# A decoder layer: the context's maxima, its rounding jobs and the zero fill are dealt out to other steps of the attention

## The reference, cut to what matters

```python
x = x + attn(layernorm(x))            # 32 query heads, 8 key/value heads, causal, rotary
x = x + xattn(layernorm(x), ctx)      # below
x = x + moe(layernorm(x))             # top-1 of 8 experts with a capacity, and a shared expert

def xattn(x, weight):                 # E, M, K = 4, 512, 512
    # both operands are rounded to 8 bits and back before the product
    xq = per 1x128 block:   (x * 448/amax).astype(fp8) * amax/448
    wq = per 128x128 block: (w * 448/amax).astype(fp8) * amax/448
    return einsum("emk,enk->emn", xq, wq)
```

## Time and profile before

| | |
|---|---|
| median of 3 runs | 1606.17 us (1605.36 to 1607.48) |
| the profiled execution | 1609.08 us |
| its span, first to last instruction | 1607.3 us |
| mean granted TensorE clock | 0.963 |
| PE busy | 1460.3 us (91%) |
| DVE busy | 1202.9 us (75%) |
| ACT busy | 949.2 us (59%) |
| POOL busy | 1020.0 us (63%) |
| `masked` of step 0 / 15 / 16 begins at | 58.97 / 171.20 / 186.14 us |
| `masked` of step 45 / 119 / 124 begins at | 402.00 / 966.26 / 1000.05 us |

### The profile page before, as it was taken

The page is one execution under the profiler, slowest core; times in us unless marked ns, Lnnn a source line. Parts: engine busy times, 40 slices in busy tenths (PEclk is TensorE's granted clock), DMA queues, the critical chain, the costliest instruction groups (busy, mean ns, idle before and its releaser), DMA issues.

```text
span 1607.3 us, 26926 instructions
## 1 busy us (share of the span) xinstructions
PE 1460.3 (91%) x8616; PEld 1276.6 (79%) x8616; DVE 1202.9 (75%) x2951; ACT 949.2 (59%) x2384; POOL 1020.0 (63%) x1007
## 2 busy tenths in 40 slices
PE   5689899999998999999999998666989898899997
PEld 4468788888877888888888887556888887899996
DVE  6678688888877778877878878976767664687785
ACT  2367677877766687878877877523121213566662
POOL 1677688988966788888888877632313132344455
PEclk8899999999999999999999999897899999899998
DMA  5654243344332334334334433012010002577767
GB/s 195 179 157 148 61 116 112 85 120 125 81 104 50 78 86 126 91 93 120 99 93 112 110 79 109 14 55 86 27 27 27 7 27 97 175 232 224 229 215 236
DMA packets 106588, 177.04 MB, mean 110 GB/s; under 512 B 16662, under 2 KB 38422, under 8 KB 106448
## 3 DMA queue, kind: packets, MB, share of 16 engines
q1 hardware_dynamic: 103888, 167.07, 35.9%
q0 software_dynamic: 2560, 8.25, 1.6%
HBM read 97.28 MB, written 31.98 MB: 80 GB/s over the span
## 4 chain that ended last, share of the span: by engine, by line
PE 66%; DVE 15%; ACT 7%; issue 5%; POOL 3%; DMA 2%; SPq 1%; DVEq 0%; POOLq 0%; ACTq 0%
PE bank L411 14%; PE bank L412 14%; PE bank L413 14%; PE bank L453 6%; PE bank L429 4%; PE bank L468 4%; PE bank L469 4%; PE bank L430 4%; ACT P L756 3%; PE bank L403 2%; DVE P L1033 2%; DVE Opair L1068 1%; ACT xnx L778 1%; ACT Otmp L762 1%; DVE work L981 1%
## 5 line engine op out<-in xcount | busy, mean ns | idle before, releaser
L756 ACT ACTIVATE P<-P,mn 128x512 f32<-128x512 f32 (+3 forms) x512 | 284.9, 557 | 220.7 <-DVE mn L1033 217.1
L1440 POOL TENSOR_TENSOR P<-P,ri 128x128 f32<-128x128 f32 (+3 forms) x512 | 358.9, 735 | 38.1 <-DVE ri L1022 31.1
L1033 DVE CUSTOM_DVE_ANT_0 P<-bank,mask 128x512 f32<-128x512 f32 (+3 forms) x512 | 236.3, 480 | 111.7 <-PE bank L430 109.3
L1074 DVE TENSOR_TENSOR PTl<-bank,PTh 128x512 fp32r<-128x512 f32 (+1 forms) x384 | 229.4, 598 | 32.9 <-ACT PTh L768 30.4
L429 PE MATMUL bank<-KT,QT 128*128 128x256 f32 (+2 forms) x512 | 190.2, 372 | 24.2 <-DVE mn L1033 23.2
L453 PE MATMUL bank<-ident,P 128*128 128x128 f32 x1280 | 203.3, 274 | 1.1 <-POOL P L1440 1.1
L768 ACT ACTIVATE PTh<-bank 128x512 fp32r<-128x512 f32 (+1 forms) x384 | 197.5, 515 | 5.6 <-PE bank L453 2.7
L411 PE MATMUL bank<-XT,Wh 128*128 128x512 f32 x384 | 165.2, 430 | 12.0 <-DVE qcs L1046 6.9
L468 PE MATMUL bank<-PTh,VS 128*128 128x256 f32 (+2 forms) x512 | 163.2, 329 | 13.3 <-DVE PTl L1074 8.6
L430 PE MATMUL bank<-KT,QT 128*128 128x256 f32 (+2 forms) x512 | 167.1, 326 | 0.0
L469 PE MATMUL bank<-PTl,VS 128*128 128x256 f32 (+2 forms) x512 | 156.5, 327 | 0.0
(11 more groups left out here) (194 smaller groups left out, 4226.0 us busy)
## 6 DMA issues: line engine op xcount, KB each, us to landing
RW<-in_wf SPq DMA_DIRECT2D x170, 256.0 KB, 3.2
QT<-qh SPq DMA_DIRECT2D x256, 64.0 KB, 2.0
QT<-ql SPq DMA_DIRECT2D x256, 64.0 KB, 2.0
Oraw<-in_wo SPq DMA_DIRECT2D x16, 512.0 KB, 5.1
xnx<-in_ctx SPq DMA_DIRECT2D x32, 256.0 KB, 3.5
KT<-KT SPq DMA_DIRECT2D x32, 256.0 KB, 3.0
Wraw<-in_wqkv SPq DMA_DIRECT2D x9, 768.0 KB, 4.7
saved<-Wh SPq DMA_DIRECT2D x7, 768.0 KB, 3.9
```

The lines of the kernel that those rows point to most:

```text
L756: e.activation(pq, pq, ACT.Exp, bias=mn[:, z, qb:qb + 1], scale=-1.0, accum_out=rs[:, z, qb:qb + 1]).then_inc(a_exp, 1)
L1033: e.tensor_tensor_reduce(P[:, z, off[qb]:off[qb] + k], bank[n % 2][:, 0:k], mask[:, 512 - k:512], -0.125, BIG, ALU.add, ALU.min, mn[:, z, ...
L1074: e.tensor_tensor(pt_part(PTl, part), bank[2 + part][:, 0:128 * n].rearrange("p (m n) -> p m n", n=128), pt_part(PTh, part).bitcast(F32), ...
L1440: e.tensor_tensor(pq, pq, ri[:, z, qb:qb + 1].to_broadcast([128, n]), ALU.mult).then_inc(g_norm, 1)
```

## The change

The steps of the maxima come from a new table: 3, 4, 5, 11, 12, 13, 19, 20, 21, 27, 28, 29, 35, 36, 37 and 43. The reduction moves from step 15 to step 45 and the scales from step 16 to step 49. The sixteen rounding jobs begin in steps 61, 65, ... 121. The zero fill is one store in each of the steps 8 to 23. `RW` is now allocated ahead of `work`, so it lies over `xnx`, `Wraw` and the first third of `Wh`, and `work` over the rest of `Wh`, `Wl`, `qcs` and half of `q2s`; the waits of both follow. The first six loads of the ring move from step 122 to step 128 behind the store of the last job, and the first three loads of kept tiles from step 114 to step 120.

```diff
+def maxima():
+    return [8 * (m // 3) + 3 + m % 3 for m in range(NCTX)]
+
 def background():
-    return [17 + 8 * j if j < 4 else 45 + 4 * j for j in range(NCTX)]
+    return [61 + 4 * j for j in range(NCTX)]
...
+        RW = sb("RW", [128, NR, 512])
         work = sb("work", [128, 8, 512])
-        RW = sb("RW", [128, NR, 512])
...
+        takes = {at: m for m, at in enumerate(maxima())}
...
                 if t >= 2 * TB:
                     need.wait_ge(p_xt, t - 1)
-                    need.wait_ge(d_keep, 64)
...
             def cross_round(b, i):
-                if t == 0:
-                    wait_wraw(need, NSAVE)
-                elif t < 3:
+                if t < 3:
                     need.wait_ge(p_kv, NU)
+                    need.wait_ge(g_ql, NU)
...
-                if -2 <= h < NCTX - 2:
-                    context_max(h + 2)
-                if h == 16:
+                if h in takes:
+                    context_max(takes[h])
+                if h == 49:
                     context_scales()
...
-                if h == 15:
+                if h == 45:
                     need.wait_ge(v_cmax, NCTX)
                     e.partition_all_reduce(...)
...
             def load_cw(t):
                 need.wait_ge(d_keep, 16 * (t + 1))
                 if t < 3:
-                    need.wait_ge(d_keep, 16 * NCTX)
-                    wait_wraw(need, NSAVE)
+                    need.wait_ge(p_kv, NU)
...
             def load_piece():
                 if j < NR:
                     need.wait_ge(p_kv, NU)
-                    need.wait_ge(g_ql, NU)
+                    need.wait_ge(d_keep, 16 * NCTX)
...
-                if h == -4:
+                if h == 0:
                     load_background(0)
                     load_background(1)
-                if -1 <= h < NCTX - 3:
-                    load_background(h + 3)
+                if takes.get(h - 1, NCTX) < NCTX - 2:
+                    load_background(takes[h - 1] + 2)
...
-                if -3 <= h < 5:
-                    for i in range(2):
-                        need.wait_ge(g_zero, 1)
-                        e.dma_start(xdz[2 * (h + 3) + i], Zb[:, 0, :]).then_inc(d_zero, 16)
-                if h == NH - 14:
+                if 8 <= h < 24:
+                    need.wait_ge(g_zero, 1)
+                    e.dma_start(xdz[h - 8], Zb[:, 0, :]).then_inc(d_zero, 16)
+                if h == NH - 8:
                     for t in range(3):
                         load_cw(t)
-                if h == NH - 6:
+                if h == NH:
                     for _ in range(NR):
                         load_piece()
```

More of the change, by code:

```diff
@@ L1671, in load_background @@
             def load_background(m):
-                if 2 <= m < NCTX + 2:
+                if 2 <= m < NCTX:
                     need.wait_ge(v_cmax, m - 1)
-                elif m == NCTX + 4:
+                elif NCTX <= m < NCTX + 2:
                     need.wait_ge(p_xt, NT)
-                elif m >= NCTX + 2:
+                elif m > NCTX + 1:
                     need.wait_ge(d_keep, 16 * (m - NCTX - 1))
```

## The result

The changed kernel takes 1611.55 us, the kernel before 1607.63 in the same comparison (11 runs of each): ratio 1.0029, interval 1.0020 to 1.0038. It is slower by 0.3%, about 4 us, where 7.5 less was forecast. The profiled execution after took 1612.85 us, with a span of 1611.0 (1607.3 before).

The account below looks back on a forecast made before the run. TensorE bounds the steady part, VectorE the loop's end; the start leaves TensorE idle. Terms -1.8 - 1.6 - 5.5 - 0.4 + 0.3 + 1.5 = -7.5 gave 1601.6 us profiled, 1598.7 median; 8-in-10 range 1591 to 1607.

Parts of the forecast that it names:

- the term of the reduction: Moving the reduction from step 15 to 45: 9.8 us at the new place against 10.2 at the old, -0.4.
- Rival B: GpSimd's way back from the reduction costs nothing at its new place: 1589.2 us, chance 0.09.
- The end: From step 119 on, late rounding jobs on VectorE and ScalarE cost +1.5 us, with 0 and 5 as ends.
- Rival C: From step 119 the loop's end is one chain; jobs cost 14.0 us instead of 1.5: 1611.2 us, chance 0.08.
- The start: Steps -4 to 10: -1.8 for maxima, -1.6 for SP's queue, -5.5 for steps 1 to 10; together -8.9 us.
- The landing of `krot`: Steps -4 to -1: without two context tiles behind it, this transfer lands sooner and GpSimd's chain starts 1.6 us earlier.
- The three maxima: Steps -2 to 0: three maxima gone from VectorE's path, 0.6 us each, -1.8 us.
- Steps 1 to 10: Three maxima instead of ten, fewer waits for context tiles: -5.5 us, with 3 and 8 as ends.
- Rival A: The start is not paced by VectorE, so only 1.8 us is left there: 1605.8 us, no change; chance 0.15.
- The middle: Maxima in steps 11 to 43 lie in the steady part and are mostly covered: +0.3 us, with 0 and 2.
- The signs named for a wrong forecast: Mask of step 15 not at least 5 us earlier, or step 119 to the loop's end growing by more than 5.
- The mask of step 119: Sign for the profile after: this mask at about 957, 9 us sooner than 966.26.

Follow-up runs that it names:

- nored: Changed kernel with a plain GpSimd addition of the same 128x64 numbers in place of the reduction over the partitions: 1596.01 us, ratio 0.9925.
- one_input_late: Changed kernel with a one-input maximum in place of VectorE's weight split of step 48, and the scales moved from step 49 to 53: 1605.57 us, ratio 0.9994.
- yield_split: Changed kernel with GpSimd waiting in step 48 until VectorE's weight split is done, and the scales moved to step 53: 1607.16 us, ratio 0.9998.
- red47: Changed kernel with the reduction in step 47 instead of 45 and the scales in step 51: 1605.21 us, ratio 0.9983.
- red23: Changed kernel with maxima in steps 3-5 and 10-22, reduction 23, scales 27, four rounding jobs at 29-41, twelve at 61-105: 1606.54 us, ratio 0.9996.
- tensor_max31: Maxima over partitions by TensorE and VectorE in steps 30/31, tile maxima denser, scales 33, jobs at 33, 37, 41 and 61-109: 1599.53 us, ratio 0.9951.
- red47_jobs35: red47 with denser rounding jobs, at steps 61, 64, 68, 71, ... 113 instead of every fourth step to 121: 1612.75 us, ratio 1.0039.
- max_early: Changed kernel with the sixteen maxima back in steps -2 to 13 and their tiles loaded from step -4 on: 1622.68 us, ratio 1.0108.
- one_input: Changed kernel with a one-input maximum over the raw weights in place of VectorE's weight split of step 48: 1605.80 us, ratio 0.9991.
- tensor_max: Changed kernel with the maxima over the partitions taken by TensorE and VectorE in steps 46 and 47, without GpSimd's call: 1600.17 us, ratio 0.9948.
- red49: Changed kernel with the reduction in step 49 instead of 45 and the scales in step 53: 1608.23 us, ratio 1.0006.
- red44: Changed kernel with the reduction in step 44 and the scales in step 48: 1610.38 us, ratio 1.0024; its profiled execution took 1604.94.

## Why the prediction was wrong

*The step that failed* is the term of the reduction: "Together 9.8 against 10.2: -0.4". Its working holds as far as it goes. GpSimd was gone 13.1 us (13.3 forecast), TensorE stood 6.46 for the probabilities (7.4), and a half clock followed. But I wrote that the jobs' two missing instructions "let GpSimd catch up", and took the catching up for harmless. It is the harm: for 17 us GpSimd leaves no gap, VectorE's split falls into it and takes 6.46, the scales 4.5 (1.9 in nored). Measured: 17.0 us by the pair nored and changed kernel, 7 more than forecast. The mask of step 48 divides it. It comes 23.2 us behind that of step 45 in nored, 30.8 in one_input_late, where the split cannot stand, and 36.8 in the changed kernel. So the absence alone cost 7.5, less than the 9.8 forecast, and the split's stand 6.1, which the forecast put at nothing; the other 3.4 come in step 49, most of them at the scales. yield_split, which takes 3.7 of the 6.1 back by a pause of GpSimd, shows that they go with VectorE's stand, red47 that they depend on where the splits lie. In the kernel before, the split of step 16 began at 178.13, before GpSimd was back, and VectorE then stood for the result itself, so nothing fell into the catching up. Rival B (way back free) is refuted by the 6.71.

*The end* was forecast as 1.5 with 0 and 5 as ends, and is 5.2. 1.8 of it come before step 119, where the forecast had nothing. The other 3.4 lie in steps 122 (1.3), 123 and 125 (1.0 each). For step 122 the rows above show the step that failed: I priced the sum of the work and took ScalarE's idle time as cover, but VectorE waits 0.84 us for ScalarE's group that had only just begun: order, not load. Steps 123 and 125 and those before 119 I did not follow. That the whole goes with the latest jobs, three kernels show: where the last job begins in step 105 (red23), 109 (tensor_max31) or 113 (red47_jobs35), steps 109 to 127 take 134.1 to 134.3 us. Rival C had this mechanism and its place, and a price of 14.0, nearly three times too high. Its time, 1611.2, lies beside the measured 1611.55 by luck: it has nothing lost at the reduction. No case had the reduction and the end costlier together, which is what happened.

*The start* came out right in sum (-9.5 by step 15 against -8.9) by luck, from two wrong parts. The landing of `krot` did not become shorter: GpSimd's wait for it is 3.28 where it was 3.38, so the two context tiles were not what made it slow. The three maxima are gone (-1.8), but 1.07 of it was lost in this execution to an instruction that met GpSimd's:

```profile
56.37 1.24 DVE L979 SCALAR_TENSOR_TENSOR rstd<-rtmp,rstd 128x8 f32<-128x8 f32 x1
```
```profile
56.33 1.25 POOL L1462 TENSOR_TENSOR krot<-krot,ksin 64x512 f32<-64x512 f32 x1 [1.64 <-DMA krot<-kvs]
```

That is the same mechanism in small, in a trace whose kernel before had rows of it too (1.2 instead of 0.7 us at the splits). One execution says little here: the eleven other kernels that have this start reach the first mask at 57.0 to 59.0 us, the middle one at 57.6, 1.4 before the kernel before. Steps 1 to 10 gave 10.0, not 5.5: I counted the tile waits only (7.3 of 9.0 are gone) and left out the seven maxima's own 0.6 each, 4.2, in a stretch in which VectorE's time is time. Rival A is refuted by max_early.

*The middle*, +0.3, was +1.2, within its ends. *Step 56* shows 1.5 us more with the same instructions in a window with a clock of 0.86 where it was 1.00; one_input, yield_split, max_early and tensor_max show the same 1.5, red49 has the like in step 54, red47, red44 and nored have it nowhere. Why the clock falls there is open.

The signs named for a wrong forecast did not catch it: the mask of step 15 was 9.45 earlier, and the loop's end grew by less than 5 from step 119 on (3.4 by step 127). The mask of step 119, forecast at 957, came at 968.

## What to carry to other kernels

An engine's absence has two prices: what waits for it, and what its catching up blocks. Before a long call is moved onto a side engine, list what the neighbour that shares its SBUF ports issues in the stretch after the return, and move either; or let the side engine pause for one instruction. If one call makes an engine leave for 13 us, try the same work on engines that are there: with two short stands of TensorE it cost 3.3 us here, where the call cost 10 to 12 at its better places (steps 15, 23 and 47) and 17.0 at the one chosen. And where engines hand over in a chain, look for the wait that a job puts into the order, besides its busy time.

## What the runs showed that I had not expected

- An instruction of VectorE stood over several of GpSimd's: 6.46, 6.40 (max_early), 7.89, 6.83 and 4.51 us in five executions, each ending within 0.6 us of the moment at which GpSimd had nothing more to do. A pause of 0.63 us was enough to end it.
- It is not always so. In other places the same kinds got through behind a single instruction of GpSimd, though the next followed without a gap: the scales after 1.94 us in red49, the splits after 1.2 to 1.3 in many steps. What decides is open.
- The kinds that stood: `TENSOR_TENSOR` and `SCALAR_TENSOR_TENSOR` with two SBUF inputs and `TENSOR_SCALAR` from SBUF to SBUF, down to 128x8 and 128x64 elements. Those that did not, beside a busy GpSimd: `TENSOR_REDUCE` (0.66), `RECIPROCAL` of 128x64 (0.55) and, with one input in a bank, `TENSOR_TENSOR` (0.67) and the masks (0.68).
- The reduction over the partitions is 0.54 us in the profile, and 13 to 14 us of absence each time: idle 5.5 to 6.0 ahead of it and 6.7 to 7.8 behind, in eleven traces.
